# Graph network on one core: ScalarE makes two of the eight pair one-hots of a pass, and VectorE merges three small steps

## What is computed

```
# layer 0, per edge e with source s and destination d
msg   = sum_b w_comp[etype,b] * (x[s] @ weight[b])
a     = tanh(relu(<x[s] @ A1 + b1, x[d] @ A2 + b2 + rel_emb[etype]> / sqrt(32)))
nei   = segment_sum(a * msg, d);  curr = x[src[last edge of d]] @ self_loop
x     = layernorm(x + relu(nei + curr))
# layer 1
x     = layernorm(x + segment_sum(x[src], dst))
# layer 2: attention with a softmax over the edges of a destination
x     = layernorm(x + segment_sum(x[src] * softmax(leaky(s_src[src] + s_dst[dst])), dst))
# layer 3: ten steps of propagation
f     = 0.9 * dst_norm * segment_sum((f * src_norm)[src], dst) + 0.1 * x   (10 times)
out   = layernorm(x + f)
```

## Time and profile before

| what | value |
|---|---|
| median of 3 runs | 1147.88 us (1146.41 to 1151.34) |
| profiled execution | 1148.57 us, its span 1146.8 us |
| busy, share of the span | PE 77%, DVE 81%, ACT 44%, POOL 53% |
| gathers on POOL | 568, 606.8 us busy, 1068 ns each |
| tanh of pass 0, of pass 97 | 71.91 us, 805.58 us |
| end of the sweep | about 812 us |

### The profile page before, as it was taken

One profiled execution on the slowest core, in us unless ns is written; L12 is line 12 of the kernel. 1 busy time (PEld: TensorE's weight loads), 2 busy tenths in 40 slices (PEclk: granted clock), 3 DMA queues, 4 the chain that ended last, 5 costly groups with the idle time before them and its releaser, 6 DMA issues.

```text
span 1146.8 us, 56069 instructions
## 1 busy us (share of the span) xinstructions
PE 883.4 (77%) x23682; PEld 838.9 (73%) x23682; DVE 933.5 (81%) x2369; ACT 504.8 (44%) x1244; POOL 608.6 (53%) x580
## 2 busy tenths in 40 slices
PE   2358887978686868777867768688468958999996
PEld 2357877877686867776767667587467958999996
DVE  8869999998898989898888988798557995555556
ACT  1135555554454546566756566556567400000000
POOL 5777777777777777777777777774000000000000
PEclk9569999888888888888988897978578979999998
DMA  4432333332232333232323322320000000000001
GB/s 117 60 75 55 64 59 60 66 57 51 48 60 54 57 52 59 52 57 57 57 56 56 51 54 50 68 45 13 5 2 3 4 2 4 5 4 4 4 5 19
DMA packets 54917, 47.97 MB, mean 42 GB/s; under 512 B 35966, under 2 KB 45182, under 8 KB 54662
## 3 DMA queue, kind: packets, MB, share of 16 engines
q0 software_dynamic: 18176, 9.34, 10.3%
q1 hardware_dynamic: 30822, 14.16, 6.1%
q10 hardware_dynamic: 5664, 20.84, 4.9%
HBM read 41.98 MB, written 2.31 MB: 39 GB/s over the span
## 4 chain that ended last, share of the span: by engine, by line
POOL 42%; DVE 19%; PE 18%; issue 16%; DMA 2%; ACT 2%; DVEq 0%; SPq 0%; ACTq 0%
POOL arena L631 42%; PE ps L883 14%; DVE arena L1372 2%; DVE arena L1612 2%; PE ps L854 2%; PE ps L893 2%; DVE arena L1411 2%; DVE arena L1632 1%; ACT arena L1120 1%; DMA arena<-line_table 1%; DMA arena<-rel_rows_in 1%; DVE aggT L1424 1%; DVE arena L1362 1%; PE ps L816 1%; DVE arena L1387 0%
## 5 line engine op out<-in xcount | busy, mean ns | idle before, releaser
L631 POOL DMA_INDIRECT arena<-x_pad,arena x568 | 606.8, 1068 | 173.4 <-issue 172.5
L816 PE MATMUL ps<-aggT 128*128 128x128 f16 x3024 | 217.3, 238 | 1.6 <-DVE aggT L1424 1.3
L816 PEld LDWEIGHTS ps<-aggT 128*128 128x128 f16 x3024 | 205.6, 110 | 3.1 <-DVE aggT L1424 3.1
L1372 DVE TENSOR_SCALAR arena<-pair_no,arena 128x275 bf16<-128x275 f16 (+2 forms) x784 | 183.1, 292 | 0.0
L883 PE MATMUL ps<-arena,adj_words 128*128 128x64 f16 x5625 | 171.9, 192 | 3.4 <-DVEq L1697 3.2
L883 PEld LDWEIGHTS ps<-arena,adj_words 128*128 128x128 fp8e4 x5625 | 170.5, 97 | 4.7 <-DVEq L1697 3.6
L1411 DVE TENSOR_TENSOR arena<-ps,arena 128x1536 f32<-128x1536 f32 x98 | 171.6, 1751 | 0.6
L1073 ACT ACTIVATE adj_words<-arena 128x500 uint8 x196 | 126.5, 646 | 56.5 <-ACT arena L1048 54.2
L1043 ACT ACTIVATE arena<-ps 128x500 fp8e4<-128x500 f32 x196 | 113.0, 577 | 86.9 <-PE ps L765 86.7
L758 PE MATMUL ps<-arena 128*128 128x25 bf16 x195 | 36.5, 187 | 148.7 <-DVE arena L1372 148.3
L778 PE MATMUL ps<-arena 128*32 128x44 f32 (+4 forms) x7048 | 131.3, 212 | 17.6 <-DVE arena L1411 17.5
(11 more groups left out here) (221 smaller groups left out, 1160.6 us busy)
## 6 DMA issues: line engine op xcount, KB each, us to landing
arena<-line_table ACTq DMA_DIRECT2D x48, 344.0 KB
arena<-x_pad,arena POOLq DMA_INDIRECT x568
arena<-pick_table SPq DMA_DIRECT2D x27, 256.0 KB
arena<-line_table ACTq DMA_DIRECT2D x48, 80.0 KB
arena<-dst_parts SPq DMA_DIRECT2D x196, 5.7 KB
agg_table<-arena SPq DMA_DIRECT2D x196, 2.5 KB
dst_parts<-aggT SPq DMA_DIRECT2D x1, 735.0 KB, 12.7
x<-x_pad SPq DMA_DIRECT2D x1, 400.0 KB
```

Source lines behind the costliest of these rows:

```text
L631: pool.indirect_dma_start(to, None, table, bass.IndirectOffsetOnAxis(ap=index, axis=0)).then_inc(done, 16)
L816: mm = nc.tensor.matmul(ps[:, at:at + PICK_WIDE * FEAT], pick_hot[:, u % PICK_RING, k * P:(k + 1) * P], x_parts[:, t, j * PICK_WIDE:(j + 1 ...
L1372: last = v.tensor_scalar(pair_hot[:, d % 2, k, 0:n], pair_no[:, 0:n], pair_of[:, d * DUO + k // SLOTS, k % SLOTS:k % SLOTS + 1], None, ALU ...
```

## The change

Three edits, all in the sweep, and their preparation:

1. The pair one-hots of slot 0 of both groups (200 columns each) go from VectorE to ScalarE. As ScalarE has no compare, it makes them in two steps: the square of (one number per partition minus `pair_no`), then relu(1 - square). `count` on TensorE now waits for both engines.
2. The last-edge marks are made together with the weighting. The destination one-hots hold two numbers for each place (destination, and destination if it is a last edge), `weight_e` holds (1, weight), and one product writes the mark and the weight into `mixed`. `make_last` falls away. The max(0, .) moves to ScalarE, as a Relu after the tanh.
3. The picked rows are summed over their four parts by one reduction in place of two additions.

```diff
@@ ScalarE
+                def make_first_pairs(d):
+                    if d >= 2:
+                        act.wait_ge(pairs_used, (d - 1) * DUO)
+                    n = PAIR_DSTS[0] * BLOCKS
+                    for g in range(DUO):
+                        last = a.activation(pair_far[:, g, :], pair_no[:, 0:n], ACT.Square, scale=-1.0,
+                                            bias=pair_of[:, d * DUO + g, 0:1])
+                    last.then_inc(first_far, 1)
+                    act.wait_ge(first_far, d + 1)
+                    a.activation(pair_hot[:, d % 2].rearrange("p (g k) v -> p g k v", g=DUO)[:, :, 0, 0:n], pair_far, ACT.Relu,
+                                 scale=-1.0, bias=ones[:, 0:1]).then_inc(first_pairs, 1)
...
                 load_lines(act, 2)
+                make_first_pairs(0)
                 for g in range(DUO):
                     copy_counts(g)
                 for d in range(DUOS):
                     act.wait_ge(score_ready, d + 1)
-                    a.activation(weight_e[:, d % 2, :], score[:, d % 2, :], ACT.Tanh, scale=1.0 / sqrt(FEAT))                     .then_inc(weight_ready, 1)
+                    a.activation(score[:, d % 2, :], score[:, d % 2, :], ACT.Tanh, scale=1.0 / sqrt(FEAT)).then_inc(tanh_made, 1)
+                    act.wait_ge(tanh_made, d + 1)
+                    a.activation(weight_e[:, d % 2, :, 1], score[:, d % 2, :], ACT.Relu).then_inc(weight_ready, 1)
+                    if d + 1 < DUOS:
+                        make_first_pairs(d + 1)
                     if d >= 1:
                         copy_sums(d - 1)
@@ TensorE, count(g)
                     if k0 == 0:
                         pe.wait_ge(pairs_ready, g // DUO + 1)
+                        pe.wait_ge(first_pairs, g // DUO + 1)
@@ VectorE, preparation
-            link(v.scalar_tensor_tensor(out=last_off_1, in0=dst_off, scalar=1.0, in1=last_off_1, op0=ALU.add, op1=ALU.mult))
+            link(v.scalar_tensor_tensor(out=off_twice[:, :, :, 0], in0=dst_off, scalar=1.0, in1=last_off_1, op0=ALU.add,
+                                        op1=ALU.mult))
+            link(v.tensor_scalar(off_twice[:, :, :, 1], dst_off, 1.0, None, ALU.add))
...
+                link(v.memset(weight_e, 1.0))
@@ VectorE, sweep
                 def make_dst_hot(c):
-                    n = [P, LINE * SLOTS, HOTS]
+                    n = [P, LINE * SLOTS, HOTS, 2]
...
-                    for k in range(k0, k1):
+                    for k in (k for k in range(k0, k1) if k % SLOTS):
...
-                def make_last(d):
...
+                    n = [P, WIDE, HOTS, 2]
+                    step(v.tensor_tensor(mixed[:, d % 2, :, :, BASES:BASES + 2], weight_e[:, d % 2].unsqueeze(2).to_broadcast(n),
+                                         dst_hot[:, d // LINE_DUOS % 2, at:at + WIDE], ALU.mult))
...
-                def add_halves():
...
+                def add_picked(c):
                     chain.wait()
                     dve.sem_inc(pick_read, 1)
-                    step(v.tensor_tensor(picked_of[:, :, 0:half], picked_of[:, :, 0:half], picked_of[:, :, half:PICK_WIDE], ALU.add))
-
-                def add_pairs(c):
-                    chain.wait()
-                    step(v.tensor_tensor(xp[:, PICKED[c] % AHEAD, :, 0:FEAT], picked_of[:, :, 0, :], picked_of[:, :, 1, :], ALU.add))
+                    step(v.tensor_reduce(xp[:, PICKED[c] % AHEAD, :, 0:FEAT],
+                                         picked.rearrange("p (k w f) -> p k f w", k=WIDE, w=PICK_WIDE), AX.X, ALU.add))
```

More of the change, by code:

```diff
@@ L244, in gnn @@
         hot_no = sb("hot_no", [P, HOTS], BF16)
-        next_no = sb("next_no", [P, HOTS], BF16)
+        next_no = sb("next_no", [P, HOTS, 2], BF16)
         pick_no = sb("pick_no", [P, PICK_DEEP])
@@ L268, in gnn @@
         start_g = old.cut(BLOCKS * FEAT).rearrange("p (b f) -> p b f", b=BLOCKS)
-        ARENA = 23880
+        ARENA = 23840
         arena = sb("arena", [P, ARENA])
@@ L275, in gnn @@
         base_t = stay.cut(GROUPS + 1, I32)
-        pair_of, dst_off, last_off_1 = [stay.cut(GROUPS * SLOTS).rearrange("p (g k) -> p g k", k=SLOTS) for _ in range(3)]
+        pair_of = stay.cut(GROUPS * SLOTS).rearrange("p (g k) -> p g k", k=SLOTS)
+        off_twice = stay.cut(2 * GROUPS * SLOTS, BF16).rearrange("p (g k i) -> p g k i", k=SLOTS, i=2)
         row_twice = stay.cut(2 * GROUPS * SLOTS, BF16).rearrange("p (g k i) -> p g k i", k=SLOTS, i=2)
@@ L295, in gnn @@
         dst_t, next_t = [of.bitcast(I32).rearrange("p (g k) -> p g k", k=SLOTS) for of in (dst_words, next_words)]
+        dst_off, last_off_1 = [prep.cut(GROUPS * SLOTS).rearrange("p (g k) -> p g k", k=SLOTS) for _ in range(2)]
         block_of = prep.cut(GROUPS * SLOTS, I32).rearrange("p (g k) -> p g k", k=SLOTS)
@@ L313, in gnn @@
         lines = sweep.cut(LINE_BUFS * LINE * WINDOW, BF16, n=SIDE).rearrange("p (h e) -> p h e", h=LINE_BUFS)
-        score, weight_e = [sweep.cut(2 * WIDE).rearrange("p (h k) -> p h k", h=2) for _ in range(2)]
-        dst_hot = sweep.cut(2 * LINE * SLOTS * HOTS, BF16).rearrange("p (h k d) -> p h k d", h=2, d=HOTS)
-        weighted = sweep.cut(WIDE * HOTS).rearrange("p (k d) -> p k d", k=WIDE)
+        score = sweep.cut(2 * WIDE).rearrange("p (h k) -> p h k", h=2)
+        weight_e = sweep.cut(2 * WIDE * 2).rearrange("p (h k i) -> p h k i", h=2, i=2)
+        dst_hot = sweep.cut(2 * LINE * SLOTS * HOTS * 2, BF16).rearrange("p (h k d i) -> p h k d i", h=2, d=HOTS, i=2)
         product = sweep.cut(WIDE * SCORED).rearrange("p (k f) -> p k f", k=WIDE)
         pair_hot = sweep.cut(2 * WIDE * HOTS * BLOCKS, BF16).rearrange("p (h k v) -> p h k v", h=2, k=WIDE)
+        pair_far = sweep.cut(DUO * PAIR_DSTS[0] * BLOCKS, BF16).rearrange("p (g v) -> p g v", g=DUO)
         row_hot = sweep.cut(2 * WIDE * P, BF16).rearrange("p (h k v) -> p h k v", h=2, k=WIDE)
-        mixed = sweep.cut(2 * WIDE * HOTS * MIXES).rearrange("p (h k d m) -> p h k d m", h=2, k=WIDE, d=HOTS)
+        mixed = sweep.cut(2 * WIDE * HOTS * (MIXES + 1)).rearrange("p (h k d m) -> p h k d m", h=2, k=WIDE, d=HOTS)
         picked = sweep.cut(WIDE * PICK_WIDE * FEAT)
@@ L1456, in run_sweep @@
                     if more:
-                        make_pairs(d + 1, 0, 3)
+                        make_pairs(d + 1, 0, SLOTS)
                     scores_of(d)
                     if more:
-                        make_pairs(d + 1, 3, 6)
+                        make_pairs(d + 1, SLOTS, 7)
                     if picked_now is not None:
@@ L1465, in run_sweep @@
                     if picked_now is not None:
-                        add_halves()
+                        add_picked(picked_now)
                     if more:
-                        make_pairs(d + 1, 6, WIDE)
-                    if picked_now is not None:
-                        add_pairs(picked_now)
+                        make_pairs(d + 1, 7, WIDE)
                     if d % LINE_DUOS == 1 and c + 1 < LINES:
```

26 lines of the change are left out of this document (8 added, 18 removed).

## The result

The changed kernel takes 1198.12 us (median of 4 runs, 1197.05 to 1199.29) against 1148.3 us (4 runs): a ratio of 1.0431, 95% interval 1.0406 to 1.0457. It is 49.8 us slower. The forecast was slower, 1164 us, with a range up to 1184: the direction and the main mechanism came true, the size did not.

The account below looks back on a forecast made before the run. Gathers bound at 7.56 us a pass, with ScalarE's chain close behind and slower from pass 46. 1148.57 + 9.5 (that chain) + 7 (TensorE's low clock) = 1165, less 0.7 to the median: 1164 us; range 1140 to 1184.

Parts of the forecast that it names:

- The loop: Sweep, tanh to tanh: ScalarE's new work in series with TensorE's counts; mean pass 7.11 us without pieces, 8.15 with.
- I take a third of this: TensorE's counts and bases at low clock: 7 us taken of 20, as its longest waits, for gathered rows, go away.
- Rival C: TensorE's low clock spreads to 22% of the counts or more: 1178 us, up to 1188; chance 0.12.
- I cost it at nothing in the sum: VectorE's saving in the sweep, 0.4 us a pass, about 40 us in all, counted as zero since VectorE does not bound.
- takes about as long as both: VectorE's reduction of 1024 elements, in 27 passes, put level with the two additions and inside VectorE's spare time.
- T(0): Time of the first tanh of the sweep: forecast 72.9 us, after one more preparation step of 0.98 us.
- T(97): Time of the sweep's last tanh, pass 97: forecast 814.8 us against 805.58 before.
- up to pass 46 nothing changes: First part of the sweep: ScalarE's chain reaches pass 46 at 399.7 us, just where the gathers would put it.
- T(46): Time of the tanh of pass 46: 399.7 us by ScalarE's chain, 401.61 in the kernel before.
- tanh to first count: Piece of each pass from ScalarE's tanh to the start of TensorE's first count: forecast 1.84 us.
- first count to first read: Piece of each pass from TensorE's first count to ScalarE's first read: forecast 0.70 us odd, 1.90 even.
- Rival A: Gathers on POOL keep setting the pace and get faster, up to 5 us by chance overlap: 1140 us; chance 0.14.

Follow-up runs that it names:

- e4: Changed kernel with ScalarE's one-hots made a pass earlier, behind the copy of the sums: 1147.16 us, ratio 0.9981.
- e11: Kernel before with only the pair one-hots moved to ScalarE, made a pass early: 1141.09 us, ratio 0.9930.
- e6: Changed kernel without ScalarE's 50 pieces of the out-degrees (counts taken as zero): 1148.33 us, ratio 0.9991.
- e7: Changed kernel with 16 constant matmuls on TensorE just ahead of its wait for the pairs: 1180.38 us, ratio 1.0265.
- e3: Changed kernel with the two additions in place of the reduction: 1185.00 us, ratio 1.0313.
- e5: Changed kernel with the reduction of the picked rows behind VectorE's last compare, not ahead of it: 1183.60 us, ratio 1.0305.
- e1: Changed kernel with all eight compares of a pass back on VectorE, marks and reduction kept: 1142.11 us, ratio 0.9945.
- e2: Kernel before with only the pair one-hots moved to ScalarE: 1164.11 us, ratio 1.0148.
- e8: Changed kernel with ScalarE's one-hots a pass earlier and two additions in place of the reduction: 1141.02 us, ratio 0.9927.
- e13: Changed kernel with picked rows laid out so the reduction reads neighbours and the mask product writes with a stride: 1198.52 us, ratio 1.0414.
- e14: Changed kernel with the neighbour-reading reduction layout and ScalarE's one-hots a pass early: 1147.63 us, ratio 0.9979.
- e10: Kernel before with only the one reduction in place of the two additions: 1146.11 us, ratio 0.9959.
- e12: Changed kernel with one-hots a pass earlier, two additions, and 16 constant matmuls in TensorE's wait for the pairs: 1141.18 us, ratio 0.9924.

## Why the prediction was right in its mechanism and wrong in its size

**Right.** The prices of ScalarE's instructions: squares 446 ns (0.46), pair Relu 628 ns (0.63). The loop: the shortest passes after are 7.43 us (odd, piece), 6.39 (odd), 7.86 (even, but for pass 0; forecast 7.82), and of the 26 even ones with a piece 8 stand at 8.91 or 8.92 (8.86) and 6 more at 9.01 or 9.02. That edit 1 turns ScalarE and TensorE into one loop is shown by e4 and e11, where the same work out of the loop costs 5 us and gains 8, and by e6. VectorE's waits for gathers vanished.

**Wrong, first step: "I take a third of this".** I had worked out 20 us for the low clock in counts and bases and took 7, because TensorE's waits for gathered rows would go. VectorE's waits for them did go, but TensorE's idle time ahead of the first count rose all the same, from 148.3 to 180.0 us: 64 waits for the pair Relu, 2.1 us each in the mean and up to 4.2, are 131.3 us of it. The granted clock of the sweep hardly moved (0.90 in both up to 400 us, then 0.88 before and 0.86 after), so the slow counts did not go away, and now they were on the path. The division gives 17 us, and e7, which fills the wait, takes 18 us off the time: 14.0 in this term and 6.1 in VectorE's. Rival C had this term at its 20 us and came to 1178; what it lacked too is the next step.

**Wrong, second step: VectorE, "I cost it at nothing in the sum", and the reduction that "takes about as long as both" additions.** The pair of additions is 0.69 + 0.39 us in e3:

```profile
L1459 DVE TENSOR_TENSOR arena<-arena 128x512 f32<-128x512 f32 x27 | 18.5, 685 | 0.0
L1463 DVE TENSOR_TENSOR arena<-arena 128x256 f32<-128x256 f32 x27 | 10.4, 385 | 0.0
```

The reduction is 1.89 us, and all of it stands ahead of the last compare, where only the first addition had stood: 1.2 us later. I judged VectorE by its mean pass, with spare time. In 14 even passes it has none. The term measured 15 us. e5 and e3 bring 14.5 and 13 us of the time back, though not all of it in this term: 11.3 and 10.0 us.

**Wrong, smaller.** The count starts 0.10 us behind the pair Relu, not 0.04, which is 5 us over 97 passes; bases and counts are 0.07 us longer in even ones (3.4); T(0) was 0.9 us later than forecast. In all 40.4 us over a T(97) of 814.8, less the 7 that I had given for the clock: 33 us, the gap from 1165 to 1198.

**The early half.** I had written "up to pass 46 nothing changes", since my chain met the gathers' pace exactly at T(46). It rested on a sum of shortest passes. The measured T(46) is 18.5 us above that sum: 0.9 of it is T(0), 10.5 lie in "tanh to first count", 7.9 in "first count to first read". The mean of T(d+1) - T(d), by kind, for the 46 passes to T(46) (before, then after): even that read picks 10.32 and 8.93; other even 7.77 and 8.23; odd that read picks 7.66 and 6.77; other odd 5.28 and 6.48. So the passes that read picks became shorter, and the 34 others longer by more: they had been short enough to make good the long ones, and lost that margin. For passes with a piece, in the same order: 10.67 and 10.37, 8.31 and 9.06, 9.36 and 7.83, 5.82 and 7.63. That the ring of 11 passes of gathered rows is what let short and long passes even out is my reading; no run tests it.

**The edits do not add up.** Edit 1 costs 15 us; on top of it edit 2 costs 21 and, on both, edit 3 13. Without edit 1 the two together gain 7 (e1). A forecast edit by edit against the old bound could not find this; that of the new loop did (0.23 us a pass for the Relu), but let the gathers swallow it in half the passes.

**Rival A: gathers did get faster, and that had no say.** They became shorter, 1068 to 1029 ns, and the last one ended at 777.07, not 791.03. That is more than the 5 us that I allowed it. With edit 1 alone the mean is 1047 ns (e2), but 1058 in e11, where the same compares are gone from VectorE, so the compares are not the whole of it. The mean gather of e3, e8, e4 and e13, in this order:

```profile
L634 POOL DMA_INDIRECT arena<-x_pad,arena x568 | 594.6, 1047 | 173.4 <-issue 172.1 <-PE ps L782 1.2
```

```profile
L634 POOL DMA_INDIRECT arena<-x_pad,arena x568 | 596.0, 1049 | 173.4 <-issue 172.8 <-PE ps L782 0.6
```

```profile
L634 POOL DMA_INDIRECT arena<-x_pad,arena x568 | 585.4, 1031 | 173.4 <-issue 172.5 <-PE ps L782 0.9
```

```profile
L634 POOL DMA_INDIRECT arena<-x_pad,arena x568 | 594.8, 1047 | 173.4 <-issue 172.8 <-PE ps L782 0.6
```

From two additions to the reduction the mean falls by 18 ns twice (e3 to after, e8 to e4), 10 us of POOL's time. The Trainium skill ("SBUF — State Buffer", section "Who interferes with whom") says that a product with both inputs in SBUF holds up GpSimd's reads and a reduction never does. Gather by gather, from 80 us on, the traces agree: those that run beside the first addition for over 0.1 us take 1.23 us in e3 and 1.38 in e8, the others 1.04 and 1.03; those that run beside the reduction take 1.00 us in the changed kernel and in e4, the others 1.03. (Both kinds can also meet the row one-hots just ahead.) The means alone do not bear it out: e13 and e14 have the reduction and no additions, and stand at 1047 and 1049 ns like e3 and e8; e5 and e7, with the long reduction, stand at 1040; and in e10 the mean falls by only 4 ns, to 1064. So how much of POOL's gain is the reduction's stays open. By the intervals e1 gains 4 to 8 us and e10 3 to 6.5, so that e1 need not be more than edit 3 alone.

The Trainium skill ("ScalarE: Activation LUTs", section "Rules for kernel authors") would keep a relu on VectorE. The changed kernel is a case for the rule, e11 one against it: with the same squares and pair Relu, a pass early, it is 8 us faster than the kernel before. I take it that ScalarE made them in its waits while VectorE had two compares less; no run separates the two.

## What to carry to other kernels

When a change puts an instruction between two engines that wait for each other, cost it in every turn of that loop, and then ask whether it can be made a turn earlier: here that was worth 51 us with not one instruction fewer. Yet the work was not free: without it (e1) the kernel takes 5 us less again. Sum a loop by kinds of pass at the clock and the waits of their typical rows, not their shortest ones; slack in a mean is slack only where short passes can pay for long ones. Judge each edit against the bound that the other edits leave.

## What the runs showed of the hardware that was not expected

A VectorE operation over 1024 f32 elements pays 0.7 to 0.8 us for a stride: of 128 bytes on the input of a reduction (1.89 against 1.20 us), and of 16 bytes on the output of a product (2.02 against 1.22 us). And 16 matmuls on constants, put ahead of TensorE's wait in each pass, raised its granted clock in the sweep from 0.90 and 0.86 to 0.99 and 0.94; in the pass shown they took 1.05 us, and the kernel became 18 us faster by them. Where gathers bound (e12 against e8) a higher clock of the same kind gave nothing.
